# A four-layer graph network kernel: the first layer's weight products in fp32 or from pairs of fp16 halves

## The reference

```python
h = jnp.maximum(_layernorm(x, axis=-1), 0.0)
x = x + _L0_gnn_ref(h, edge_index, L0_gnn_W_l, L0_gnn_b_l, L0_gnn_W_r, L0_gnn_gamma, L0_gnn_beta)

def _L0_gnn_ref(x, edge_index, W_l, b_l, W_r, gamma, beta):
    agg = jax.ops.segment_sum(x[src], dst, num_segments=n)
    cnt = jax.ops.segment_sum(jnp.ones((src.shape[0],), x.dtype), dst, num_segments=n)
    mean_agg = agg / jnp.maximum(cnt, 1.0)[:, None]
    h = mean_agg @ W_l.T + b_l + x @ W_r.T
    mu = jnp.mean(h, axis=0)
    var = jnp.var(h, axis=0)
    h = (h - mu) * jax.lax.rsqrt(var + EPS) * gamma + beta
    return jax.nn.relu(h) + x
```

## Time and profile before

| | |
|---|---|
| median of 3 runs | 1223.15 us (1222.41 to 1226.34) |
| profiled execution | 1222.51 us, its span 1220.8 us |
| TensorE busy | 1125.2 us, 92% of the span |
| DVE, ACT, POOL busy | 902.2 us (74%), 716.0 us (59%), 65.0 us (5%) |
| mean granted TensorE clock | 0.967 of full speed |
| aggregation, then products of the first layer | 146.27 to 196.49 us, then 67.49 us |

### The profile page before, as it was taken

One profiled execution on the slowest core, in us unless ns is written; L12 is line 12 of the kernel. 1 busy time (PEld: TensorE's weight loads), 2 busy tenths in 40 slices (PEclk: granted clock), 3 DMA queues, 4 the chain that ended last, 5 costly groups with the idle time before them and its releaser, 6 DMA issues. The chain is left out here.

```text
span 1220.8 us, 16229 instructions
## 1 busy us (share of the span) xinstructions
PE 1125.2 (92%) x5960; PEld 709.9 (58%) x5960; DVE 902.2 (74%) x1654; ACT 716.0 (59%) x901; POOL 65.0 (5%) x117
## 2 busy tenths in 40 slices
PE   6999999978989968889999999979999999999996
PEld 5666655547765543344454444436557777777775
DVE  6999940127558795978989997955458888888885
ACT  2325772025558664068887777735147777777774
POOL 3000141000002000000000000000000000000000
PEclk9999999989999978979999999979999999999999
DMA  4000000030030001104111100000021101111002
GB/s 159 5 1 1 0 2 1 1 112 26 1 95 3 1 0 50 61 1 149 45 45 45 45 24 3 1 1 1 6 48 27 28 1 27 28 28 27 2 1 85
DMA packets 24771, 36.18 MB, mean 30 GB/s; under 512 B 11874, under 2 KB 13204, under 8 KB 24694
## 3 DMA queue, kind: packets, MB, share of 16 engines
q1 hardware_dynamic: 24694, 35.14, 9.5%
HBM read 26.03 MB, written 2.70 MB: 24 GB/s over the span
## 5 line engine op out<-in xcount | busy, mean ns | idle before, releaser
L63 PE MATMUL wide<-arena 125*125 125x512 bf16 (+5 forms) x2076 | 457.5, 369 | 13.6 <-DVE arena L962 6.0
L63 PEld LDWEIGHTS wide<-arena 125*125 125x125 bf16 (+5 forms) x2076 | 250.9, 130 | 193.5 <-issue 76.2
L1789 PE MATMUL wide<-arena 125*65 125x512 f32 (+1 forms) x480 | 181.2, 514 | 0.0
L1390 PE MATMUL wide<-ident,arena 125*125 125x125 f32 (+3 forms) x954 | 131.4, 285 | 12.5 <-ACT arena L619 4.7
L759 ACT ACTIVATE arena<-arena,b 125x1250 f32<-125x1250 f32 x80 | 106.7, 1336 | 59.1 <-PE wide L1789 54.8
L1283 DVE TENSOR_TENSOR arena<-wide,arena 125x1250 f32<-125x1250 f32 x80 | 116.7, 1458 | 29.7 <-PE wide L1779 29.5
L1390 PEld LDWEIGHTS wide<-ident,arena 125*125 125x125 f32 (+3 forms) x954 | 116.1, 187 | 22.6 <-issue 9.4
L842 ACT ACTIVATE arena<-wide 125x1000 f16<-125x1000 f32 x80 | 80.8, 1010 | 79.8 <-PE wide L1390 79.8
L1789 PEld LDWEIGHTS wide<-arena 125*65 125x65 f32 x480 | 63.1, 138 | 101.0 <-issue 94.6
L1349 DVE SCALAR_TENSOR_TENSOR arena<-wide,arena 125x1000 f16<-125x1000 f32 x80 | 95.9, 1198 | 33.8 <-ACT arena L842 33.8
L857 ACT ACTIVATE arena<-arena,neg_max,unit 125x1250 f32<-125x1250 f32 x80 | 114.3, 1429 | 5.7 <-DVE neg_max L1376 5.7
(11 more groups left out here) (257 smaller groups left out, 1249.5 us busy)
## 6 DMA issues: line engine op xcount, KB each, us to landing
arena<-rows_kept SPq DMA_DIRECT2D x16, 625.0 KB, 6.1
arena<-arena SPq DMA_DIRECT2D x40, 156.2 KB, 2.8
arena<-in_L_gnn_W SPq DMA_DIRECT2D x3, 1024.0 KB, 8.3
x_nm<-in_x SPq DMA_DIRECT2D x2, 1250.0 KB
out<-x_nm SPq DMA_DIRECT2D x1, 2187.5 KB
arena<-in_L_gnn_W_l SPq DMA_DIRECT2D x1, 1024.0 KB, 5.4
arena<-in_L_gnn_W_r SPq DMA_DIRECT2D x1, 1024.0 KB, 7.9
arena<-in_L_gnn_Wk SPq DMA_DIRECT2D x1, 1024.0 KB, 5.3
```

The source lines that it names most:

```text
L63: mm = pe.matmul(ps[0:rows, lo:hi], lhsT, rhs[:, lo:hi], start=start, stop=stop, skip_group_check=True)
L1390: return pe.transpose(dst, src, ident[0:k, 0:k])
L1789: m = pe.matmul(psW[1][0:VA, lo:hi], v_gat[0:ROWS, t, h, :], ring[n % RINGS][0:ROWS, lo:hi], start=(t == 0), stop=(t == TILES - 1))
```

## The change

The three operands of the first layer's weight products become pairs of fp16 halves, and each fp32 product becomes three fp16 products, added in the same PSUM bank: upper with upper, upper weight with lower data, lower weight with upper data.

- The turned weights are scaled so that the largest is 2^14 (`fit0`), and split by `weights_first` (ACT) and `weights_rest` (DVE). The largest weight comes from two passes of ACT over `w_nat` and a maximum over partitions on POOL.
- h is turned from its halves: `turn_pair`, eight 16-bit matmuls a tile against `ident_bf`, behind the tiles 0, 2, 4, 6, 8 of blocks 1 and 2. Both halves go to PSUM together, the upper to `psS[0]`, the lower to `psS[1]`, and `turned_pair` (DVE) copies both.
- A block of the aggregation goes to `agg_one`, from which ACT takes the upper half (`agg_upper`) and DVE the lower. The factor 1/2048 leaves `rdeg_b` and goes into the scale of ACT's evacuation, and for the second layer into `scl1`.
- ACT widens seven tiles of a block and POOL three, in both layers. POOL adds four tiles of h to x in a block.
- `yT` of the first layer and the weights of the second layer's queries and keys get places of their own (`w_query`, `w_key`).

The core of the diff:

```diff
-        yT = region(G + 5000, [KD, N])
+        yT = [region(o, [KD, N]) for o in (G + 9396, G + 5000)]
+        hT_pair = [region(6250 + 2500 * i, [KD, N], F16) for i in range(2)]
+        agg_pair = [region(G + 2500 * i, [KD, N], F16) for i in range(2)]
+        agg_one = region(12500, [N])
+        w_pair = [[region(G + 5000 + 1024 * (2 * i + j), [KD, D], F16) for j in range(2)] for i in range(2)]
+        w_key, w_query = [region(G + 4608 + 2048 * i, [KD, D]) for i in range(2)]
...
-        BY_ACT = (0, 2, 3, 4, 5, 7, 8, 9)
-        BY_POOL = (1, 6)
+        BY_ACT = (0, 2, 3, 5, 6, 8, 9)
+        BY_POOL = (1, 4, 7)
...
+            pool.wait_ge(S["w_maxed"], 1)
+            pool.partition_all_reduce(w_all[:, 0:2], w_most[:, 0:2], 128, RMAX).then_inc(S["w_spread"], 1)
             pool.wait_ge(S["counts_turn_read"], 3 * TILES - 2)
             for k in range(KD):
                 widen(0, k)
-                for t in range(3 * k, min(3 * k + 3, TILES)):
+                for t in range(4 * k, min(4 * k + 4, TILES)):
...
+            for i in range(2):
+                m = act.activation(w_nat[i], w_nat[i], ACT.Abs, accum_out=w_most[:, i:i + 1])
+            m.then_inc(S["w_maxed"], 1)
...
+            def weights_first(i):
+
+                act.activation(w_pair[i][0], (w_a, w_b)[i], ACT.Copy, scale=fit0[:, 0:1]).then_inc(S["w16_hi"], 1)
+
+            def agg_upper(k):
+
+                act.wait_ge(S["agg_taken"], k + 1)
+                copy(agg_pair[0][:, k, :], agg_one).then_inc(S["agg_hi"], 1)
...
+                        if l == 0 and k >= 1 and j == BY_ACT[3]:
+                            agg_upper(k - 1)
...
+                    if l == 0 and k >= 2:
+                        if k == 2:
+                            act.wait_ge(S["fit_set"], 1)
+                            act.wait_ge(S["x_plus_h"], TILES)
+                        weights_first(3 - k)
...
             big = widen(0)
+            agg_upper(KD - 1)
             act.wait_ge(S["vec_in"], 16 * 10)
-            act.wait_ge(S["x_plus_h"], TILES)
             for f in range(KD):
                 act.wait_ge(S["y_full"], f + 1)
-                act.activation(yT[:, f, :], psW[f % 2][:, 0:N], ACT.Identity, bias=bl_c[:, f:f + 1]).then_inc(S["y_out"], 1)
+                act.activation(yT[0][:, f, :], psW[f % 2][:, 0:N], ACT.Identity, bias=bl_c[:, f:f + 1],
+                               scale=fit0[:, 1:2]).then_inc(S["y_out"], 1)
...
+            def turned_pair(t):
+
+                dve.wait_ge(S["h_turned"], t + 1)
+                for part in range(2):
+                    m = dve.tensor_copy(hT_pair[part][:, :, t * ROWS:(t + 1) * ROWS], psS[part][:, 0:KD * ROWS].rearrange("p (k c) -> p k c", k=KD))
+                m.then_inc(S["hT_made"], 1)
+
+            def weights_rest(i):
+
+                dve.wait_ge(S["w16_hi"], 2 - i)
+                stt(w_pair[i][1], (w_a, w_b)[i], fit0[:, 0:1], w_pair[i][0], ALU.mult, ALU.subtract).then_inc(S["w16_lo"], 1)
...
-                tt(aggT[:, k, :], psW[k % 2][:, 0:N], rdeg_b, ALU.mult).then_inc(S["agg_taken"], 1)
-                if k == 0:
-                    for t in range(TILES):
-                        turned_tile(0, t)
-                if k == 1:
-                    done(ts(pos_b, rdeg_b, MOST_DEG * HS, 1.0, ALU.mult, ALU.min))
+                after(dve, "agg_read", k)
+                tt(agg_one, psW[k % 2][:, 0:N], rdeg_b, ALU.mult).then_inc(S["agg_taken"], 1)
+                if k < 2:
+                    for t in range(HEAD_HALF * k, HEAD_HALF * k + HEAD_HALF):
+                        turned_pair(t)
+                        if k == 0 and t == 0:
+                            dve.wait_ge(S["w_spread"], 1)
+                            most = w_all[:, 2:3]
+                            done(tt(most, w_all[:, 0:1], w_all[:, 1:2], ALU.max))
+                            done(ts(most, most, LEAST, 1.0 / TOP16, ALU.max, ALU.mult))
+                            done(ts(fit0[:, 1:2], most, 1.0 / HS, None, ALU.mult))
+                            dve.reciprocal(fit0[:, 0:1], most).then_inc(S["fit_set"], 1)
+                if k == KD - 1:
+                    weights_rest(1)
+                dve.wait_ge(S["agg_hi"], k + 1)
+                tt(agg_pair[1][:, k, :], agg_one, agg_pair[0][:, k, :], ALU.subtract).then_inc(S["agg_read"], 1)
+            weights_rest(0)
+            dve.wait_ge(S["agg_read"], KD)
+            done(ts(pos_b, rdeg_b, MOST_DEG, 1.0, ALU.mult, ALU.min))
...
-                bn_over_nodes(hT, lambda f: dve.wait_ge(S["hT_made"], TILES * 2), g1_c, b1_c, scl1, shf1)
+                done(bn_over_nodes(hT, lambda f: dve.wait_ge(S["hT_made"], TILES * 2), g1_c, b1_c, scl1, shf1))
+                ts(scl1[:, :], scl1[:, :], 1.0 / HS, None, ALU.mult)
...
+            def turn_pair(t):
+
+                after(pe, "hT_made", t)
+                for part in range(2):
+                    for k in range(KD):
+                        m = pe.matmul(psS[part][:, k * ROWS:(k + 1) * ROWS], h_pair[part][0:ROWS, t, 128 * k:128 * k + 128],
+                                      ident_bf[0:ROWS, 0:ROWS], start=True, stop=True)
+                m.then_inc(S["h_turned"], 1)
...
-                        if l == 0 and k == 1:
-                            turn_h(0, j)
+                        if l == 0 and k in (1, 2) and j % 2 == 0:
+                            turn_pair(HEAD_HALF * (k - 1) + j // 2)
...
+                if f == 0:
+                    pe.wait_ge(S["hT_made"], TILES)
+                    pe.wait_ge(S["w16_lo"], 1)
                 for k in range(2 * KD):
-                    w, r = ((w_b, hT), (w_a, aggT))[k // KD]
+                    if f == 0 and k >= KD:
+                        pe.wait_ge(S["agg_read"], k - KD + 1)
                     if f == 0 and k == KD:
-                        pe.wait_ge(S["agg_taken"], KD)
-                    m = wide_matmul(pe, psW[f % 2], 128, w[:, k % KD, 128 * f:128 * f + 128], r[:, k % KD, :], k == 0, k == 2 * KD - 1)
+                        pe.wait_ge(S["w16_lo"], 2)
+                    w, r = ((w_pair[1], hT_pair), (w_pair[0], agg_pair))[k // KD]
+                    for i, (w_part, r_part) in enumerate(((w[0], r[0]), (w[0], r[1]), (w[1], r[0]))):
+                        m = wide_matmul(pe, psW[f % 2], 128, w_part[:, k % KD, 128 * f:128 * f + 128], r_part[:, k % KD, :],
+                                        k == 0 and i == 0, k == 2 * KD - 1 and i == 2)
```

More of the change, by code:

```diff
@@ L150, in gnn_program @@
         w_all = sb("w_all", [128, 3])
+        fit0 = sb("fit0", [128, 2])
         fit = sb("fit", [128, 3])
@@ L309, in gnn_program @@
             counts_turn_read deg_split deg_turned deg_row_out deg_wide ln_ready h_made h_turned hT_made
-            x_plus_h h1_made h_split cT_wide cT_used cP_wide lo_wide lo_made lo_used agg_full agg_taken agg_read w_turned
+            x_plus_h h1_made h_split cT_wide cT_used cP_wide lo_wide lo_made lo_used agg_full agg_taken agg_hi agg_read w_turned
             w_turn_read y_full y_out y_stats y_scaled y_started z_turned x_updated  qk_full qk_out v_full v_out
@@ L388, in _ @@
             sp.wait_ge(S["y_full"], KD)
-            sp.dma_start(w_b, a["L1_gnn_Wk"].rearrange(rows, p=128)).then_inc(S["w_in"], 16)
-            sp.dma_start(w_a, a["L1_gnn_Wq"].rearrange(rows, p=128)).then_inc(S["w_in"], 16)
+            sp.dma_start(w_key, a["L1_gnn_Wk"].rearrange(rows, p=128)).then_inc(S["w_in"], 16)
+            sp.dma_start(w_query, a["L1_gnn_Wq"].rearrange(rows, p=128)).then_inc(S["w_in"], 16)
             sp.dma_start(wv, a["L1_gnn_Wv"].rearrange(rows, p=128)).then_inc(S["wv_in"], 16)
@@ L575, in scale_y @@
                     for f in range(blocks):
-                        act.activation(yT[:, f, nodes], yT[:, f, nodes], ACT.Identity, bias=shf[:, f:f + 1],
+                        act.activation(yT[l][:, f, nodes], yT[l][:, f, nodes], ACT.Identity, bias=shf[:, f:f + 1],
                                        scale=scl[:, f:f + 1]).then_inc(S["y_scaled"], 1)
@@ L630, in weights_up @@
                 if half == 0:
-                    act.wait_ge(S["fit_set"], 1)
+                    act.wait_ge(S["fit_set"], 2)
                 k = slice(KD // 2 * half, KD // 2 * half + KD // 2)
@@ L735, in _ @@
                 act.wait_ge(S["agg_full"], 2 * KD)
-                act.wait_ge(S["agg_read"], KD)
+                act.wait_ge(S["agg_read"], 2 * KD)
                 for f in range(KD):
@@ L740, in _ @@
                     act.wait_ge(S["conv_full"], f + 1)
-                    act.activation(yT[:, f, :], psW[f % 2][:, 0:N], ACT.Relu, bias=bc_c[:, f:f + 1]).then_inc(S["conv_out"], 1)
+                    act.activation(yT[1][:, f, :], psW[f % 2][:, 0:N], ACT.Relu, bias=bc_c[:, f:f + 1]).then_inc(S["conv_out"], 1)
                 take_root(128, 0, KD)
                 act.wait_ge(S["y_stats"], 2)
-                scale_y()
+                scale_y(1)
             if layers >= 3:
@@ L1063, in _ @@
```

(10 more changed lines are left out.)

22 lines of the change are left out of this document (11 added, 11 removed).

## The result

The changed kernel takes 1221.89 us (median of 20 runs, 1218.21 to 1224.21), the kernel before 1225.3 us in as many runs beside it (1222.41 to 1230.35). The ratio is 0.997, with a 95% interval of 0.9962 to 0.9978. That is 3.4 us between the medians and 3.7 us by the ratio, at the very bound of what I called a difference, where 8.3 us were forecast. The forecast's interval, 1210 to 1220 us, misses the median. Of that miss 2.1 us come from the median of before, which was 1223.15 us in three runs and 1225.3 us in twenty; the rest is a gain that isn't there.

The account below looks back on a forecast made before the run. TensorE alone was taken to bound the first layer from 159 to 264 us. Terms -15.8 + 3.9 + 1.6 + 0.9 + 0.6 + 0.4 + 0.1 = -8.3 us gave a 1214.9 us median, range 1210 to 1220 us.

Parts of the forecast that it names:

- What bounds the kernel: First layer, 159 to 264 us: the path is TensorE alone, so shorter products shorten the program and its waits lengthen it.
- The product: First layer's weight products: 288 fp16 matmuls in 51.6 us replace 67.49 us of fp32; -15.8 us, firm to 0.3.
- The wait at its start: Ahead of the weight products, TensorE waits for DVE's last-block multiplication and weights_rest(1); +3.9 us, between 3.6 and 4.1.
- The clock behind it: Behind the wait ahead of the products, the clock falls to 1.2 GHz; +1.6 us, ends 0 and 3.3.
- The turning: Ten turns by eight 16-bit matmuls replace ten by four fp32 transposes, 0.52 against 0.43 us each; +0.9 us.
- A queue on DVE: Seam of blocks 1 and 2: TensorE waits before pair 6 while DVE works through its queue; +0.6 us, 0 to 2.
- Shares: ACT, held by row_sb, widens tile 6 late, so TensorE waits; +0.4 us. Later ACT work is covered by four buffers.
- The rest: Passes over w_nat and POOL's maximum cost 0, hidden in idle time; scl1 instruction 0.1 us; other items 0.
- four signs of being wrong: Product wait above 5 us, turns over 0.7 us each, ACT making TensorE wait in block 3, or later layers lengthening.
- its length for block 1, 13.5 us: Expected length of aggregation block 1 in the changed kernel's profile, with block 2 at 14.1 us.
- The rival of DVE and POOL holding each other up: DVE lower halves and POOL casts and additions slow each other in three places; about +3 us, 1218 us; chance 0.15.
- The clock staying low through the products: Slow case: 1.2 GHz persists in the weight products, up to 1265 us if over all of them; chance 0.04.

Follow-up runs that it names:

- e2: Changed kernel with DVE's two weights_rest moved ahead by one place; 1214.95 us, ratio to the kernel before 0.9918.
- e9: e1 with weights_rest for w_b split into two instructions, the products starting behind the first; 1214.99 us, ratio to the kernel before 0.9922.
- e1: Changed kernel plus a spare memset and tensor_tensor on POOL right behind the early maximum over partitions; 1215.55 us, ratio to the kernel before 0.9922.
- e8: e7 with block 2's five turns one tile later, behind the odd tiles; 1208.58 us, ratio to the kernel before 0.9867.
- e7: e3 with tile 6 for POOL and tile 7 for ACT; 1208.12 us, ratio to the kernel before 0.9864.
- e3: Changed kernel with both edits, those of e1 and e2; 1211.05 us, ratio to the kernel before 0.9886.
- e4: Kernel before plus only ACT's two passes over w_nat and POOL's maximum, result unused; 1228.49 us, ratio to the kernel before 1.0035.

## Why the prediction was wrong, step by step

- **What bounds the kernel**: right. From 146 to 262 us TensorE is the path; each us that it stood or gained there moved the turn back.
- **The product, -15.8 us**: right. Without a wait in front it takes 51.30 us, 0.178 us a matmul, so -16.2, a little outside the 0.3 us that the term was said to be firm to.
- **The wait at its start, +3.9 us**: right, 3.90 us, by the very instructions named: the multiplication of 1.46 and weights_rest of 2.34 us.
- **The clock behind it, +1.6 us**: right in the mechanism (e2, e9); 1.6 us in the changed kernel's trace and in e9, 2.5 in e1. The size hit the first of these, but the spread between 1.6 and 2.5 behind the same wait says that it could have come out otherwise.
- **The turning, +0.9 us**: too dear. A turn takes 0.44 us (161.62 to 162.06 in e1), 0.43 before: +0.1 us. The nearest row, L1467's 0.065 us a matmul, was no measure of it: eight in 0.44 us are 0.055 each. The Trainium skill's sustained figure of about 81 ns for each 128-column matmul (TensorE: Matmul & The Clock Gate, Back-to-back issue gap) is further off; the measurement decides.
- **A queue on DVE, +0.6 us**: right, 0.50 us, and e8 shows the cause.
- **Shares, +0.4 us**: right, 0.41 us, and e7 shows the cause. That ACT would not be late: right.
- **The rest, "POOL's maximum over partitions follows there. Costing 0"**: this is the step that failed. The maximum was hidden, but its second half, POOL's return to tensor_tensor, was not there: it fell at the next tensor_tensor, in block 0. It cost 4.04 us of wait and 2.8 us of low clock in block 1's row, 5.7 us in e1's trace, 6.3 us in e1's median. With it the sum would have been about -8.3 + 6.8 = -1.5 us, and with 0.8 less for the turns and 0.4 less for the product -2.7, against -3.7 measured by the ratio (-4.7 to -2.7). Where the last us lies stays open: later layers differ between traces by up to 2 us with the clock. That the turns and the product were both too dear by the forecast made its miss 1.2 us smaller, which is luck. None of the four signs of being wrong that the forecast named came, since none of them asks for POOL's own queue; only its length for block 1, 13.5 us against 19.91, shows the miss.
- **The rival of DVE and POOL holding each other up** named the right symptom, a late cast of POOL, but with 3 us where 6.8 were paid, and by a mechanism that was not the cause: in e1 the same instructions run side by side and block 1 has no wait. Instructions that lengthen each other do stand in the changed kernel, off the path: the last lower half but one takes 2.28 us where its like take 1.45, when POOL's cast had just started. In e1 and e3 the same pair of instructions gives 2.28 us again.

```profile
198.72 2.28 DVE L1134 TENSOR_TENSOR arena<-arena 128x1250 f16<-128x1250 f32 x1 [1.68 <-ACT arena L554]
```

```profile
198.46 1.23 POOL L487 CAST arena<-cntT 125x1250 f16<-125x1250 int16 x1 [1.90 <-PE wide L63]
```

- **The clock staying low through the products**: did not occur in any of the traces.

## What to carry to other kernels

A step on POOL costs more than its own row: when the kind of instruction changes to or from a maximum over partitions, look for MODIFY_POOL_CONFIG in its queue, count some 7 us for it in each direction (6.5 to 7.5 us here), and place both where POOL owes nobody anything; a spare instruction of the next kind is enough to place the return. Where TensorE is the path, price a wait by its length and the low clock behind it (2.84 us standing cost 1.6 more in e9, 1.97 us in e4 nothing more), and look at the engine's idle time just before the wait for the work that it waits for: moving two instructions by one place brought the turn back 5.8 us forward (e2). Read every row that a change adds to an engine's order, also the ones without operands.

## What the runs showed of the hardware that I had not expected

- POOL's change to the maximum over partitions and back takes 6.7 to 7.5 us on the way there and 6.5 to 7.5 us on the way back over the eleven traces that have it, at 21 us and at 153 us alike, while casts and a memset right behind the maximum run without it.
- The same wait of 3.36 us ahead of the second aggregation was followed by the 1.2 GHz level in the trace of before and not in that of the changed kernel (60 matmuls in 12.46 and in 10.81 us). A single trace can't tell which of the two a run gets.
- Eight 16-bit matmuls of 125 columns, each with weights of its own, take 0.44 us, as long as four fp32 transposes of the same tile.
